# Two packed attentions: fills taken out of the norms, less work on VectorE, and two heads of the unmasked one on the two halves of the array's rows

## The reference

```
x = x + L0_xattn(ctx, layernorm(x), mask, ...)     # 8 heads of 16, masked
x = x + L0_ffn(layernorm(x), ...)                  # 4 rounds, 4 experts, top 2
x = x + L1_xattn(layernorm(x), ctx, ...)           # 16 heads of 8, no mask
x = x + L1_ffn(...)  ... five more updates of the same form

# L1_xattn
q, k, v = split(x @ w_qkv.T)                        # (4, 16, 256, 8) each
k = concat([ctx_k, k]); v = concat([ctx_v, v])      # 512 keys per sequence
attn = softmax((q * 8 ** -0.5) @ k.T)
out  = (attn @ v) @ w_proj.T + b_proj
```

## Time and profile before

| | |
|---|---|
| median of 3 runs | 1290.31 us (1285.53 to 1293.37) |
| the profiled execution's own time | 1288.04 us |
| its span, first to last instruction | 1286.2 us |
| TensorE busy | 1104.2 us, 86% of the span |
| VectorE busy | 812.3 us, 63% |
| ScalarE busy | 676.8 us, 53% |
| GpSimd busy | 406.6 us, 32% |
| mean granted TensorE clock | 0.925 of 2.4 GHz |

### The profile page before, as it was taken

How to read it: one execution, slowest core, us unless ns; L and a number is a source line. 1 busy time by engine, 2 the same in 40 slices (tenths; PEclk the granted TensorE clock), 3 DMA queues, 4 the chain that set the end, 5 groups by cost and what they waited for, 6 DMA issues and landing times.

```text
span 1286.2 us, 18277 instructions
## 1 busy us (share of the span) xinstructions
PE 1104.2 (86%) x6234; PEld 778.7 (61%) x6234; DVE 812.3 (63%) x1962; ACT 676.8 (53%) x1601; POOL 406.6 (32%) x576
## 2 busy tenths in 40 slices
PE   3587899999739998778989999967999799998777
PEld 2346677777513444656667777745777567675665
DVE  6865687888668783577766776665211366666464
ACT  2154566676414556366767787752333256666022
POOL 7401111111530000235556776673100144444200
PEclk8598899999967999898989999986999899999979
DMA  5301000000022400300000000305000100000000
GB/s 208 99 27 55 1 1 1 1 1 1 1 82 61 169 21 1 132 0 1 1 1 1 1 1 1 131 18 218 1 1 1 67 1 2 1 2 1 1 1 18
DMA packets 24733, 42.75 MB, mean 33 GB/s; under 512 B 3616, under 2 KB 22336, under 8 KB 23360
## 3 DMA queue, kind: packets, MB, share of 16 engines
q1 hardware_dynamic: 24640, 41.58, 9.2%
HBM read 36.94 MB, written 4.46 MB: 32 GB/s over the span
## 4 chain that ended last, share of the span: by engine, by line
PE 68%; DVE 15%; ACT 8%; issue 3%; POOL 2%; SPq 2%; DMA 1%; DVEq 0%; ACTq 0%; POOLq 0%
PE psum L1071 7%; PE psum L1442 7%; PE psum L1061 5%; PE psum L813 5%; PE psum L823 4%; ACT region_d L1508 4%; PE psum L346 3%; PE psum L2075 3%; PE psum L2052 2%; PE psum L1429 2%; PE psum L319 2%; PE psum L2019 2%; PE psum L2036 2%; PE psum L2014 2%; PE psum L1479 2%
## 5 line engine op out<-in xcount | busy, mean ns | idle before, releaser
L1442 PE MATMUL psum<-gated_parts 128*128 128x512 f32 x768 | 198.4, 413 | 16.6 <-DVE region_d L1613 15.7
L1442 PEld LDWEIGHTS psum<-gated_parts 128*128 128x128 f32 x768 | 142.6, 193 | 68.3 <-DVE region_d L1613 33.0
L1682 POOL TENSOR_TENSOR region_d<-region_d 128x256 f32<-128x256 f32 x128 | 101.8, 796 | 119.0 <-DVE region_d L1613 117.6
L1146 ACT ACTIVATE rounds_work<-psum,region_c 128x512 f32<-128x512 f32 x128 | 86.9, 689 | 59.8 <-PE psum L1061 59.8
L132 POOL TENSOR_TENSOR rstd<-var_eps,minus_half 128x4 f32<-128x4 f32 x16 | 16.3, 1020 | 282.8 <-DVE var_eps L92 280.7
L1613 DVE SCALAR_TENSOR_TENSOR region_d<-psum,ctx,region_d 128x128 f32<-128x128 f32 x256 | 71.8, 344 | 43.1 <-ACT region_d L1508 39.6
L1508 ACT ACTIVATE region_d<-psum,gated_work 128x128 f32<-128x128 f32 x256 | 75.1, 439 | 44.9 <-issue 26.2
L1071 PE MATMUL psum<-parts,split 128*128 128x512 f32 x384 | 97.8, 404 | 0.0
L1061 PE MATMUL psum<-parts,split 128*128 128x512 f32 x384 | 94.7, 397 | 0.0
L675 DVE TENSOR_REDUCE work<-psum 128x1 f32<-128x512 f32 x128 | 82.3, 684 | 18.5 <-PE psum L308 17.7
L1302 POOL CAST parts<-rounds_work 128x1024 fp32r<-128x1024 f32 x32 | 33.3, 1041 | 183.9 <-ACT rounds_work L1146 183.9
(11 more groups left out here) (377 smaller groups left out, 2318.1 us busy)
## 6 DMA issues: line engine op xcount, KB each, us to landing
region_a<-in_l1v SPq DMA_DIRECT2D x1, 4096.0 KB, 15.1
region_b_last<-in_l1o SPq DMA_DIRECT2D x1, 4096.0 KB, 12.0
region_a<-in_l2f SPq DMA_DIRECT2D x1, 4096.0 KB, 13.7
region_b_last<-in_l3f_small SPq DMA_DIRECT2D x1, 4096.0 KB, 19.8
region_a<-in_l3f SPq DMA_DIRECT2D x1, 2080.0 KB, 7.7
region_c<-in_l0f SPq DMA_DIRECT2D x1, 2076.0 KB, 12.1
region_c<-in_l3x SPq DMA_DIRECT2D x1, 2048.0 KB, 7.7
front_work<-q_parts SPq DMA_DIRECT2D x24, 64.0 KB
```

Of the source, the lines that this page charges most:

```text
L1146: act.activation(H[g % 2][:, f, :], bank[f], ACT.Gelu_apprx_tanh, bias=W("b1")[:, (g % E) * FT + f:(g % E) * FT + f + 1]).then_inc(h_ready ...
L1442: ins = pe.matmul(bank[2 * (n % 2) + c], src[a][:, t * P:(t + 1) * P], weights[b][:, piece(c)], start=m == 0, stop=m == len(PASSES) - 1)
L1682: pool.tensor_tensor(tile[:, 0:2, :], tile[:, 0:2, :], tile[:, 2:4, :], ALU.add).then_inc(k.pool_chain, 1)
```

## The change

For `l1x` (`masked` is false) a slot now holds two heads: one in rows 0 to 50, one in rows 64 to 114 (48 rows of terms and three of maxima), and each matmul of both passes is placed on its half of the array's rows. `place_of`, `four` and `group` order the heads so that matmuls that follow one another are on different halves and in different banks. The weights of the output projection are permuted to that order. The zero rows of the queries are gone, so QS needs no fill.

Both attentions store the parts in DRAM once for each term in which they appear, 24 transfers of 128 KB instead of 12 for q and k, and six instead of three for the context; a load is then one transfer of all terms of a head, for each side: in `l1x` two of keys, two of queries and two of context for each share (before 3, 6, 3), in `l0x` one and one (before 3, 6). `l0x` loads its mask rows first of all, each behind its fill. The maxima of `l1x` need six transfers for a unit in place of three.

The fills are written as float32 words that hold two bf16 ones, half as many elements. For `l1x` they run inside the rounds of the stage before (four, behind the casts of items 8 to 11), and its VA is filled behind the split of q and k. The split of the next stage's weights waits for `z_ready` to be 2.

In `l1x` ScalarE takes the output (as it already does in `l0x`) and the values from PSUM, GpSimd copies the context's values, and GpSimd splits the maxima, which ScalarE hands it as float32. In both, ScalarE takes the maxima ahead of the exponential of the same step.

```diff
-    R_MASK = 96
+    R_MASK = len(TERMS) * HD
+    SIDES = 1 if masked else 2
+    SIDE = P // SIDES
+    def place_of(h):
+        if masked:
+            return 0, h
+        return h % HPU // 4, h // HPU * 4 + h % 4
+    def four(hg):
+        w, x = divmod(hg, 2)
+        return [HPU * w + 4 * side + 2 * x + c for side in range(2) for c in range(2)]
+    def group(n):
+        w, n = divmod(n, GU)
+        return n // 2 % 2, [HPU * w + 4 * (n % 2) + n // 4]
...
# first pass (the second alike, with ROWS, heads in the order 0, 2, 1, 3)
-                                QS[b % BUFS][0:R_MAX, h0 + j, t * P:(t + 1) * P],
-                                KS[b % BUFS][0:R_MAX, h0 + j, :], start=True, stop=True)
+                                QS[b % BUFS][rows_at(side, R_MAX), slot, t * P:(t + 1) * P],
+                                KS[b % BUFS][rows_at(side, R_MAX), slot, :], start=True, stop=True,
+                                tile_position=(side * SIDE, 0))
...
# ScalarE
-        if masked:
-            act.wait_ge(*stored.at(16 * 12))
+        act.wait_ge(*stored.at(16 * 24))
         for i in range(ALL + LAG + 1):
+            if i % SU == 0 and 0 < i <= ALL:
+                maxima(i // SU - 1)
-            if masked and s > 0 and s % key_tiles == 0:
+            if s > 0 and s % key_tiles == 0:
+            if not masked and i % STEPS == VALUES_AT % STEPS and VALUES_AT <= i < ALL + VALUES_AT:
+                own_values((i - VALUES_AT) // STEPS)
...
# GpSimd
-            fill_queries(0)
-            fill_queries(1)
-            pool.memset(KS[0][:, :, :], 1.0).then_inc(fill_done.semaphore, 1)
             k.norm.gpsimd(pool, use)
-            pool.memset(KS[1][:, :, :], 1.0)
+            pool.wait_ge(*rest.at(8))
...
-            pool.wait_ge(*rest.at(8))
+            pool.wait_ge(ahead.z_ready, 2)
             split.gpsimd(pool)
+            return
+        def split_maxima(v):
+            pool.wait_ge(*nm_part.at(v + 1))
...
+            pool.tensor_copy(high, f).then_inc(nm_rest.semaphore, 1)
+            pool.wait_ge(*nm_rest.at(3 * v + 1))
+            chained(pool.tensor_tensor(r, f, high, ALU.subtract))
+            pool.tensor_copy(mid, r).then_inc(nm_rest.semaphore, 1)
+            pool.wait_ge(*nm_rest.at(3 * v + 2))
+            pool.tensor_tensor(low, r, mid, ALU.subtract).then_inc(nm_rest.semaphore, 1)
...
# SyncE
+                    for row in places[i]:
+                        store(dram, NH, parts[i], row, cols).then_inc(stored.semaphore, 16)
+        def load_rows(dram, dst, first, b, share, done):
+            slots = slice(share * SPS, (share + 1) * SPS)
+            for side in range(SIDES):
+                h = share * HPS + side * SPS
+                src = dram.rearrange("(h r) t -> r h t", h=NH)[:, h:h + SPS, b * S:(b + 1) * S]
+                sp.dma_start(dst[rows_at(side, R_MASK), slots, first:first + S], src).then_inc(done, 16)
...
# GpSimd in the stage before l1x
+            if FILL_AT <= g < FILL_AT + 4:
+                n = g - FILL_AT
+                pool.memset(k.later_slots[n // 2][:, n % 2 * T:(n % 2 + 1) * T], ONES_16)\
+                    .then_inc(k.slots_filled.semaphore, 1)
```

More of the change, by code:

```diff
@@ L185, in packed_attention @@
     NMp = [[k.carve(BF16, P) for _ in range(3)] for _ in range(2)]
+    NMf = [k.carve(F32, P) for _ in range(2)]
     vtmp = k.carve(F32, HALF)
@@ new lines, in load @@
+            load_rows(k_dram, KS[b % BUFS], NK - S, b, share, done)
+            load_rows(q_dram, QS[b % BUFS], 0, b, share, done)
+            if not masked and b > 0:
+                load_context(b, share)
+        if masked:
+            sp.wait_ge(k.mask_ready, 1)
+            for b in range(BUFS):
+                sp.wait_ge(*fill_done.at(b + 1))
+                sp.dma_start(KS[b][R_MASK:R_MASK + 1, :, :],
+                             k.mask_bias[0:1, b * S:(b + 1) * S].unsqueeze(1).broadcast_to([1, NH, S]))\
+                    .then_inc(loaded[b][0].semaphore, 16)
+        else:
+            sp.wait_ge(*k.slots_filled.at(4))
```

236 lines of the change are left out of this document (130 added, 106 removed).

## The result

| | |
|---|---|
| before, median of 17 runs | 1291.43 us (1285.53 to 1294.99) |
| changed, median of 17 runs | 1283.02 us (1279.64 to 1288.2) |
| ratio | 0.9943, 95% interval 0.9928 to 0.9958 |
| the changed kernel's profiled execution | 1283.63 us, span 1281.8 (1286.2 before) |
| busy: TensorE, VectorE, ScalarE, GpSimd | 1105.2, 778.8, 682.3, 395.6 us |

What follows compares the result with a forecast made beforehand. The prediction took fills colliding with the norm, then SyncE's queue, to bound the head of `l1x`, and TensorE its plain steps. Terms −10.9 + 1 − 9 + 2.5 − 1 − 1.5 = −18.9 on 1288.04 gave 1269.1, stated as 1270; range 1256 to 1283.

Steps and rivals of the forecast that it cites:

- The head of `l1x`: Start of `l1x`: without fills beside the norm, and with fewer loads, first pass at about 369.7 instead of 380.65, −10.9 us.
- Maxima of unit 0: `l1x`, after the first passes: stores and loads queued on SyncE make these maxima land at 388.8, wanted at 387.8, +1 us.
- `l0x`: Masked stage: faster products and an earlier start of their sums against GpSimd's split beside the loop; together −1.5, between −6.5 and +2.5.
- the path of the stores: `l0x`: stores issued until about 37, landed about 41; L1850 starts at 45.7 instead of 51.22, −5.5 us.
- the clash of GpSimd's split with VectorE in the loop: `l0x` main loop: about eight VectorE operations can each wait up to 2.34 us for GpSimd; 0 to 9 us, taken as 5.
- The loop and its stall: `l1x` loop: steps and extras −9 (bounds −3 and −21), weights' transfer +2.5, tail bound by ScalarE −1.
- The wait for the maxima of unit 3: `l1x` loop: these maxima queue behind `in_l1v`, 15.1 us to land, and second passes now want them at about 57 us: +2.5.
- ties in: `l1x` plain step: with halves overlapping, VectorE's reductions hold the step at 1.45 us, saving 0.10 and not 0.41.
- A: Rival, `l1x` loop: the halves don't overlap, only VectorE's relief stays, −3 for −9; 1274 us; chance 0.20.
- B: Rival: transfers become the bound; each of seven later `l1x` units 1 us late gives 1277 us; chance 0.12.
- C: Rival, `l1x` loop: no tie between engines, step falls to VectorE's 1.29 us; 1262, with extras hidden 1257; chance 0.10.
- D: Rival, `l1x` loop: idle time in each step leaves TensorE at 1.2 GHz, plain step 1.97 us, 1308 us; chance 0.05.

Runs made afterwards that it cites:

- The experiment with twelve stores: Changed kernel with the split behind the last row maxima, and in `l0x` alone twelve stores and loads by parts as before: 1276.94 us, 0.9877.
- `in_l1v` last: Changed kernel with the 4 MB transfer `in_l1v` issued behind the last unit of the unmasked attention instead of the third: 1275.75 us, 0.9877.
- the kernel with the fills a second time: Changed kernel with the four fills ahead of the unmasked attention's norm and the same four again behind the norm's roots: 1288.79 us, 0.9973.
- the experiment on that kernel: Kernel before the change with `in_l1v` issued behind the last unit of the unmasked attention instead of the third: 1290.13 us, 0.9991.
- the form tried: Changed kernel, `in_l1v` behind the last unit, output and own-value copies and the maxima split (four chained operations at once) on VectorE in `l1x`: 1291.59 us, 0.9996.

## Why the prediction was wrong

The forecast was 1270, the time 1283; the direction and the head of `l1x` were right, the terms of `l0x` and of the loop were not. The forecast's own sum also slipped: 1269.1 and the 2.3 us between the trace and the median make 1271.4 and not 1270.

*The head of `l1x`: right in size* (−10.9, measured −11.0), half right in its reason. The collision of fills and norm was the cost: fills laid beside L123 again cost 1.8 us on that line alone, and 2.3 us up to the first pass. But that they moved beside the rounds was worth nothing measurable. The prediction overlooked that fills of 3.65 us would be over before the norm if they stood ahead of it, as two of the three long ones did before.

*Maxima of unit 0: right* (+1, measured +1.2).

*`l0x`: the largest miss, +6.0 for −1.5.* Two steps failed. The first is the path of the stores. The prediction had the last ones issued by 37 and landed by 41, L1825 and L1828 over at 45.2, and L1850 at 45.7. They landed 4.8 us behind the start of the last issue, as before the change (4.9), but that issue came at 40.10: SyncE first waited until 31.46 for the first half to land and loaded, and only then stored the second. ScalarE was released at 44.91, so 5.5 us of gain became 1.9, and the first pass, which the prediction left where it was, came 4.0 us later. The experiment with twelve stores confirms it: ScalarE starts at 38.29, the first pass comes at 32.33. The second is the clash of GpSimd's split with VectorE in the loop, taken at 5 us: put back to either side of the loop the split is 3.3 to 3.8 us cheaper by the medians, 4 to 6 in the traces, though one of these places makes the eight products slow again. So the move lost more than it brought. Again a wait (3.2 us of TensorE behind L749) went on as a low clock. The low clock behind 90 us is a third loss, and its cause is open.

*The loop and its stall: mis-sized, by the clock at two places.* Here is the time between the starts of second passes, 16 steps at a time, and of what is left:

| steps | 0 to 16 | 16 to 32 | 32 to 48 | 48 to 52 | 52 to 63 | to the reciprocal |
|---|---|---|---|---|---|---|
| before | 28.02 | 28.75 | 28.75 | 6.88 | 15.25 | 3.56 |
| changed | 26.91 | 30.14 | 26.12 | 6.36 | 15.03 | 3.39 |
| `in_l1v` last | 26.84 | 26.12 | 26.12 | 6.36 | 15.03 | 3.39 |

The steady sequence came out as forecast (26.13 against 25.9 us). The wait for the maxima of unit 3 was foreseen at the right place, +2.5. The step that failed was to price that stall by its wait: the wait was 1.1 us, and with the fall to 1.2 GHz behind it the loop lost 4.1. The rest of the loop, with the transfer out of the way, gains 7.35 us (111.21 to 103.86) where −9 and −1 were forecast. The first sequence gains 1.2 us and not 2.85, and the clock rises 7 us behind the first second pass and not, as the prediction took from the kernel before, with it. Where it rose another 7.5 us later, in the kernel with the fills a second time, this sequence was 2.4 us longer, so I take the late rise for the cause. The steps from 52 on gain 0.4 in place of 1. Rows of before had shown nothing of this: the clock was at 1.00 from 400.1 us on, and the same transfer cost nothing that the experiment on that kernel could tell.

*That VectorE "ties in": not settled.* The copies, which I counted among the relief (4 × 0.41 us a sequence), show no cost on VectorE. The chain of the maxima, together with them, costs 15 us there in the form tried, more than the kernel before can have paid for its own. How the 2.6 us of a steady sequence divide between halves and relief no run here shows; that the two can be added is not shown either.

*The +2.6 behind `l1x` is not from its code.* From that stage's last addition to the end it took 757.9 us before. In the changed kernel and the fifteen others here, whose code behind that point is the same but for the place of `in_l1v`, it took 757.6 to 758.1 in five and 760.5 to 761.0 in seven, the changed kernel among them; the other four lie between 755.1 and 760.3. Both groups hold kernels with the transfer in its old place. Whether the change makes one group more likely, single traces can't tell. The two differ in the granted clock of 520 to 540 us, here of the changed kernel and of the one with `in_l1v` last:

```profile
520.00:540.00 20.00, 13.30 (x48) 0.74 0.52 211
```

```profile
520.00:540.00 20.00, 16.39 (x63) 0.83 0.39 165
```

*The rivals.* A is out: the pairs overlap. B was wrong for `l1x`: there the units' own transfers came in time in the calm stretch, and only the one of 4 MB made some of them late. In `l0x` the 24 stores did hold up the stage: with twelve the median is 2.8 us lower. C is out: the step did not fall to 1.29 us. D's price was right where its state occurs: its plain step at 1.2 GHz, 1.97 us, is 1.98 in the changed kernel's timeline, where the clock was still low:

```profile
398.45 0.64 PE L369 MATMUL psum<-work 51*128 51x256 bf16 x4
...
400.43 0.64 PE L369 MATMUL psum<-work 51*128 51x256 bf16 x4
```

What the forecast lacked was D in part: not the whole loop at the low level, but 7 us at its start and 10 us behind a stall.

The Trainium skill (TensorEngine Tiling (Array Packing), Key Properties) has the array drained at a change of the tiling mode; with the 0.1 us that the prediction took from a row for one, the gain would be about 2 us smaller. No run here isolates that drain.

## What to carry to other kernels

Shorter TensorE steps can make a wait dear that cost nothing before: here a stall of 1.1 us was followed by 10 us at 1.2 GHz and cost 4.1. Look first for long transfers on the queue ahead of short ones that TensorE waits for. Follow the list of the engine that issues transfers in order: what stands behind a wait for a landing is late by that wait too. When work is moved off one critical place, look at which engine pair it now meets, and whether TensorE waits for that engine there: beside the eight products the split held VectorE for 9 us and cost the stage less than beside the loop. Cut the work itself before you move it: the shorter fills needed no new place.

## What the runs showed of the hardware

**The clock can stay at 1.2 GHz with TensorE never idle.** With the first pass's two matmuls on one half of the rows the granted clock is 0.50 in every window from 400 to 540 us, TensorE busy for 19.95 to 20.00 of 20 us; with the same matmuls on different halves it rises 7 us after the first second pass and the kernel takes 1283 us, not 1335. The Trainium skill (TensorE: Matmul & The Clock Gate, What's actually happening) says that activity releases the throttle; the profile's busy time does not tell it here, for these traces have more of it at the low clock. Why the order of the heads decides is open: the step at the low clock is 2.40 us against 1.98, and the matmuls in it are the same.

**GpSimd holds up one-input operations of VectorE between SBUF tiles, by a fill too.** The eight L123 lengthen from 2.35 to 4.17 us beside memsets, the two L749 from 0.48 to 2.90 beside the split. The Trainium skill (SBUF — State Buffer, Who interferes with whom) says that VectorE's `tensor_scalar` can enter a mode in which it shares a pair of ports with GpSimd, and that the one which comes second is blocked for the whole instruction of the other. The trace agrees for L749: the first scaling starts 0.6 us into an L1409 and ends with it (65.13 and 65.05 us), the second ends with the L1407 behind it (66.11 and 66.03). Beside the fills no single pair was followed in this way.

**Doubled stores cost time on the queue, twice over.** The release of the wait for all stores in `l0x` moved by 6.6 us between the kernels with 24 and with 12 of them, and the last issue by 6.5; the last store lands 4.8 us behind its issue with 24 and 4.7 with 12. Of the 6.5 us, 3.0 are issues of the first half, 2.2 its later landing, for which SyncE waits, and 4.6 issues of the second half; fewer loads between give 3.3 back.
